# One decoder layer on one core: the gate and up products stand between the two halves of the value products

## The chip, the core and the metric

The kernel runs on one core of a Trainium2 chip. The metric is the time of one execution on the device, in microseconds (us); lower is better. Before the change it is 531.68 us, the median of three runs (531.52 to 532.6). The engines are PE (matrix products, with a weight load, PEld, that overlaps them), DVE (vector work), ACT (activation functions, copies out of PSUM), POOL (further elementwise work) and SP, which issues the DMAs. Each engine works through its own list of instructions in order and waits at semaphores for the others.

## The reference, cut to what matters

The layer has three blocks over 4 sequences of 1024 rows of 256 values. Each is normalised and added back to `x`: a gated linear scan, a cross attention of 16 heads over 64 context rows and one null row, and a feed-forward block with quantised activations and weights.

```python
x = x + attn(layernorm(x), w_qkva, gamma)
# cross attention: 16 heads of 64, keys and values from ctx (64 rows) and null_kv
sim  = einsum('bhid,bhjd->bhij', q * 64**-0.5, k)
attn = softmax(sim, axis=-1)
out  = einsum('bhij,bhjd->bhid', attn, v)  # heads joined, then @ Wout
x = x + (out - mean(out)) * rsqrt(var(out) + 1e-6) * ln_scale + ln_bias
# feed-forward, inner width 1024; bitlinear quantises both operands
z = layernorm(x)
gate, up = silu(bitlinear(z, w_gate)), bitlinear(z, w_up)
x = x + bitlinear(gate * up, w_down)
```

## The kernel before

The 4096 rows are 32 tiles of 128 rows. The first block runs in 4 groups of 4 tiles; then the keys are folded with Wq into `Mhi` and `Mlo`, and the values with Wout into `VW`. After that (from about 165 us in the profile) the cross attention and the feed-forward run together in one software pipeline, the function `stages2_3(n, u4)`, which every engine goes through for n = -2 to 38. In step n, PE does for five different tiles:

- `scores_half(n + 2, 0)` and `scores_half(n + 2, 1)`: the scores of tile n + 2, 12 matmuls of 260 columns each, into PSUM banks 0, 1 and banks 2, 3. (Line 1128 is the helper `group`, which also records gate, up and down.)
- The transposes of tile n's softmax weights `p2` into banks 4 and 5 (lines 1348 and 1356) and those of the null row's weights into bank 7 (line 1360).
- `gate_up(n, v)`: 4 matmuls of 512 columns with `wgT` into banks 0 and 1 (gate), 4 with `wuT` into banks 2 and 3 (up), for tile n - 5.
- The value products of tile n: 4 matmuls with `VW` (first half, line 1370), 4 more (second half, line 1375) and one for the null row (line 1378), all accumulated in bank 7. The profile shows each of the eight as two records, so a half is x8 there. The first half waits for `pT0_ready` and `pTn_ready`.
- In even steps a pair of transposes for a later tile (line 1261), then the down product of tile n - 7.

Around them stand, in the order of each engine's list:

- DVE in step n: the row maximum (line 984) and the subtraction (line 987) for each half of the scores of tile n + 2, the small part of the null weights of tile n (line 1045, which releases `pTn_ready`), the softmax sum of tile n + 1 (line 996), statistics (1060, 1068), then for tile n - 5 `hidden_layer` (line 1009: gate times up, waits for `silu_ready`, `zw_done` and `up_psum`), for tile n - 3 the maximum of the normalised rows (line 1074, waits for `z_ready`), the statistics of the attention output of tile n (line 1081, waits for `out_psum`), the maximum of the hidden layer (line 1016), small scale factors, and the residual of tile n - 7 (line 1027).
- ACT in step n: the copies of the transposed weights out of PSUM (737, 740, 742), the load of the Silu table (688), Silu of the gate product (line 693, waits for `gate_psum`), the quantised copy of the previous tile's hidden layer (755), the normalised rows of tile n - 3 (line 701, which releases `z_ready`), the load of the Exp table and the exponential (766).

The order is written out by hand; no scheduler stands behind it. Gate and up share their banks with the scores, so gate waits until DVE is done with the first half of the scores of tile n + 2 (`sim_sub`), and up until it is done with the second half.

Of the kernel before, what the change touches and what calls it, by code (L numbers as in the profile page):

```python
# [33 lines left out]
def decoder_layer(nc, x, ctx_in, w_qkva, gamma, Wq, Wkv, null_kv, Wout, ln_scale, ln_bias,  # L34
# [7 lines left out]
    T = B * N // P  # L42
# [17 lines left out]
    with ExitStack() as stack:  # L60
# [8 lines left out]
        def bank(b, n=512):  # L69
            return psum[:, b, 0:n]  # L70
# [268 lines left out]
        def positive(value):  # L339

            return not isinstance(value, int) or value > 0
# [18 lines left out]
        def exists(n, count):  # L360

            return not isinstance(n, int) or 0 <= n < count

        def upto(n, count):

            return min(n, count) if isinstance(n, int) else n

        def filling(n):

            return isinstance(n, int) and n < 1  # L370

        def late(n):

            return isinstance(n, int) and n >= T

        def half(n):
            return n >> 1

        def batch(n):
            b = n >> (TB.bit_length() - 1)  # L380
            return b if isinstance(b, int) else b.with_bounds(min_val=0, max_val=B - 1)
# [742 lines left out]
        def _(pe):  # L1124
            def group(dst, terms):

                for i, (lhsT, rhs) in enumerate(terms):
                    mm = pe.matmul(dst, lhsT, rhs, start=i == 0, stop=i == len(terms) - 1)  # L1128
                return mm
# [124 lines left out]
            def pair_T(q, r):  # L1254

                pe.wait_ge(xn2_ready, 2 * q + 2)
                if positive(q):
                    pe.wait_ge(xT2_lo_ready, q)
                for k in range(KD):
                    for t in range(2):  # L1260
                        mm = pe.transpose(psum[:, 6, k * 2 * P + t * P:k * 2 * P + (t + 1) * P],  # L1261
                                          xn2[:, 2 * r + t, k * P:(k + 1) * P], ident[:, :])
                mm.then_inc(xT2_psum, 1)
# [31 lines left out]
            def scores_half(n, hh, u4, q, b):  # L1295

                pe.wait_ge(xT2_lo_ready, q + 1)
                if n == 0 and hh == 1:
                    pe.wait_ge(vw_first, HC)
                    pe.wait_ge(vw_second, HC)  # L1300
                if positive(2 * n - 1 + hh):
                    pe.wait_ge(sim_sub, 2 * n - 1 + hh)
                if positive(n - 7):
                    pe.wait_ge((silu_ready, h_ready)[hh], n - 7)
                for g in (2 * hh, 2 * hh + 1):
                    mm = group(bank(g, HB * J),
                               [(xT[:, (u4 // 2) % 2, k, (u4 % 2) * P:(u4 % 2 + 1) * P],
                                 m[:, k, b, g * HB * J:(g + 1) * HB * J])
                                for k in range(KD) for xT, m in ((xT2hi, Mhi), (xT2hi, Mlo), (xT2lo, Mhi))])
                mm.then_inc(sim_psum, 1)  # L1310
# [7 lines left out]
            def gate_up(n, slot):  # L1318

                pe.wait_ge(nT_ready[slot], 16 * ((n - 5) // 2 + 1))  # L1320
                pe.wait_ge(sim_sub, upto(2 * n + 5, 2 * T))
                if positive(n - 5):
                    pe.wait_ge(silu_ready, n - 5)
                for j in range(2):
                    mm = group(bank(j), [(nT3[:, slot, k, :], wgT[:, k, j * 512:(j + 1) * 512]) for k in range(KD)])
                mm.then_inc(gate_psum, 1)
                pe.wait_ge(sim_sub, upto(2 * n + 6, 2 * T))
                if positive(n - 5):
                    pe.wait_ge(h_ready, n - 5)
                for j in range(2):  # L1330
                    mm = group(bank(2 + j), [(nT3[:, slot, k, :], wuT[:, k, j * 512:(j + 1) * 512]) for k in range(KD)])
                mm.then_inc(up_psum, 1)

            def stages2_3(n, u4):
                u, v = u4 % 2, 1 - u4 % 2
                if exists(n + 2, T):
                    scores_half(n + 2, 0, (u4 + 2) % 4, half(n + 2 - u), batch(n + 2))
                    if not filling(n):
                        scores_half(n + 2, 1, (u4 + 2) % 4, half(n + 2 - u), batch(n + 2))
                elif not late(n):  # L1340
                    gate_up(n, v)
                if exists(n, T):

                    pe.wait_ge(p_ready, 2 * n + 2)
                    if positive(n):
                        pe.wait_ge(pT0_ready, n)
                    for i in range(HC // 2):
                        mm = pe.transpose(psum[:, 4, i * P:(i + 1) * P], p2[:, u, i * P:(i + 1) * P], ident[:, :])
                    mm.then_inc(pT0_psum, 1)
                    if positive(n):  # L1350
                        pe.wait_ge(pT1_ready, n)
                    if positive(n - 7):
                        pe.wait_ge(x3_done, n - 7)
                    for i in range(HC // 2):
                        at = (HC // 2 + i) * P
                        mm = pe.transpose(psum[:, 5, i * P:(i + 1) * P], p2[:, u, at:at + P], ident[:, :])
                    mm.then_inc(pT1_psum, 1)
                    if positive(n):
                        pe.wait_ge(y2_ready, n)
                    pe.transpose(psum[0:NP, 7, D:D + P], p2[:, u, H * MK:], ident[:, :]).then_inc(pTn_psum, 1)  # L1360
                if filling(n):
                    scores_half(n + 2, 1, (u4 + 2) % 4, half(n + 2 - u), batch(n + 2))
                if exists(n + 2, T) and exists(n - 5, T):
                    gate_up(n, v)
                if exists(n, T):

                    pe.wait_ge(pTn_ready, n + 1)
                    pe.wait_ge(pT0_ready, n + 1)
                    for pair in range(HC // 2):
                        pe.matmul(bank(7, D), pT[:, pair, :], VW[:, batch(n), pair, :], start=pair == 0, stop=False)  # L1370
                if exists(n, T):

                    pe.wait_ge(pT1_ready, n + 1)
                    for pair in range(HC // 2, HC):
                        pe.matmul(bank(7, D), pT[:, pair, :], VW[:, batch(n), pair, :], start=False, stop=False)  # L1375
                    if n == 0:
                        pe.wait_ge(vwn_ready, 1)
                    pe.matmul(bank(7, D), pTn[:, :], VWnull[:, :], start=False, stop=True).then_inc(out_psum, 1)
                if u == 0 and exists(n, T - 4):
                    pair_T(half(n) + 2, u4 // 2)  # L1380
                if exists(n - 7, T):

                    pe.wait_ge(nhT_ready[v], 16 * ((n - 7) // 2 + 1))
                    pe.wait_ge(pT1_ready, upto(n + 1, T))
                    if positive(n - 7):
                        pe.wait_ge(x3_done, n - 7)
                    group(bank(5, D), [(nhT3[v][:, k, :], wdT[:, k, :]) for k in range(FC)]) \
                        .then_inc(down_psum, 1)
                if isinstance(n, int) and n >= T - 1 and exists(n - 4, T):
                    gate_up(n + 1, u)  # L1390

            steps(stages2_3)


# [22 lines left out]
```

## Time and profile before

| | before |
|---|---|
| time, median of 3 runs | 531.68 us |
| the profiled execution | 531.91 us |
| its span, first to last instruction | 530.1 us |
| PE busy | 477.0 us, 90% |
| DVE busy | 427.8 us, 81% |
| ACT busy | 325.1 us, 61% |
| POOL busy | 304.8 us, 57% |
| mean granted TensorE clock | 0.983 |

The span is the profiled execution without what lies ahead of its first and behind its last instruction, here 1.8 us. Busy is the time in which an engine executed something; the chain that ended last runs for 54% of the span over PE and for 30% over DVE, so neither alone sets the time. Times below are microseconds from the start of the span.

### The profile page before, as it was taken

Reading aid. Unit: us, or ns where it says so; the run is one execution under the profiler, and the core shown is the slowest. Engines: PE = TensorE matmul, PEld = TensorE weight load, DVE = VectorE, ACT = ScalarE, POOL = GpSimd, SP = SyncE. Lnnn points to the kernel's source line nnn. Section 1 sums busy time; section 2 is a strip of 40 time slices with the busy share of each in tenths; the row PEclk is TensorE's granted clock in tenths of the full one; section 3 lists DMA queues with packets and bytes.
Section 4 is the critical chain, followed back from the end, with each engine's and each line's share of the span. In section 5 each row is a group of like instructions: output and inputs, shape, how many; then the busy total and the mean of one; then the engine's idle time right before and its main releaser. Section 6 shows DMA issues by size and latency. Waiting matters only on the chain.

```text
span 530.1 us, 9241 instructions
## 1 busy us (share of the span) xinstructions
PE 477.0 (90%) x2926; PEld 389.5 (73%) x2954; DVE 427.8 (81%) x936; ACT 325.1 (61%) x450; POOL 304.8 (57%) x482
## 2 busy tenths in 40 slices
PE   1899999989988998999999999999999999998562
PEld 0676787767767887978887888888888878867221
DVE  4899998968527667889889889989898899886763
ACT  4433333236333434788878888888888788876450
POOL 2211233810001467788787787787877877888731
PEclk9989999999999999999999999999999999999995
DMA  8995000240000000011122122212221211122342
GB/s 263 324 350 215 1 0 1 40 80 1 1 1 1 1 1 6 6 31 36 37 54 49 39 47 45 51 36 53 44 46 36 55 41 46 38 53 51 70 100 69
DMA packets 68173, 32.06 MB, mean 60 GB/s; under 512 B 50720, under 2 KB 66336, under 8 KB 68128
## 3 DMA queue, kind: packets, MB, share of 16 engines
q1 hardware_dynamic: 68128, 31.50, 23.2%
q8 instruction: 23, 0.38, 0.3%
q14 instruction: 22, 0.18, 0.1%
HBM read 15.24 MB, written 4.19 MB: 37 GB/s over the span
## 4 chain that ended last, share of the span: by engine, by line
PE 54%; DVE 30%; issue 6%; POOL 4%; DMA 4%; ACT 1%; DVEq 1%; POOLq 0%
PE psum L1128 22%; PE psum L1370 10%; PE psum L1375 10%; DVE region_d L987 5%; DVE mx L984 4%; DVE amax L1016 3%; PE psum L1144 3%; DVE region_a L870 3%; DMA region_d<-region_d 2%; PE psum L1231 2%; PE psum L1248 1%; DVE st L1081 1%; DVE xs L812 1%; PE psum L1261 1%; DMA region_c<-region_d 1%
## 5 line engine op out<-in xcount | busy, mean ns | idle before, releaser
L523 POOL TENSOR_TENSOR region_d<-region_d,rden 128x1024 f32<-128x1024 f32 x32 | 60.9, 1903 | 90.5 <-DVE rden L1001 90.5
L1128 PE MATMUL psum<-Mhi,xT2hi 128*128 128x260 f32 x256 | 75.0, 293 | 0.2
L1128 PE MATMUL psum<-Mlo,xT2hi 128*128 128x260 f32 x256 | 72.4, 283 | 0.0
L1128 PE MATMUL psum<-Mhi,xT2lo 128*128 128x260 f32 x256 | 72.3, 283 | 0.0
L1370 PE MATMUL psum<-VW,region_d 128*128 128x256 f32 x256 | 61.1, 381 | 4.8 <-DVE pTn L1045 4.8
L1375 PE MATMUL psum<-VW,region_d 128*128 128x256 f32 x256 | 60.5, 379 | 0.0
L1370 PEld LDWEIGHTS psum<-VW,region_d 128*128 128x128 f32 x256 | 48.1, 190 | 14.9 <-DVE pTn L1045 6.4
L1375 PEld LDWEIGHTS psum<-VW,region_d 128*128 128x128 f32 x256 | 48.6, 190 | 6.6
L984 DVE TENSOR_REDUCE mx<-psum 128x8 f32<-128x520 f32 x64 | 44.2, 691 | 6.4 <-PE psum L1128 5.2
L1128 PEld LDWEIGHTS psum<-Mhi,xT2hi 128*128 128x128 f32 x256 | 48.2, 188 | 1.3 <-issue 1.0
L1128 PEld LDWEIGHTS psum<-Mlo,xT2hi 128*128 128x128 f32 x256 | 48.3, 189 | 0.0
L1128 PEld LDWEIGHTS psum<-Mhi,xT2lo 128*128 128x128 f32 x256 | 48.2, 188 | 0.0
L987 DVE TENSOR_TENSOR region_d<-psum,mx 128x520 f32<-128x520 f32 x64 | 44.8, 700 | 2.2
L1009 DVE SCALAR_TENSOR_TENSOR region_c<-psum,zw,region_c 128x1024 f32<-128x1024 f32 x32 | 41.0, 1282 | 3.6 <-ACT region_c L693 3.2
L489 POOL TENSOR_TENSOR pw_out<-pw_in,expo 128x8 f32<-128x8 f32 x8 | 13.1, 1641 | 52.4 <-DVE pw_in L804 52.4
L535 POOL CAST region_d<-region_c 128x1024 bf16<-128x1024 int16 x32 | 33.2, 1036 | 14.1 <-ACT region_c L755 14.1
L755 ACT ACTIVATE region_c<-region_c,qr 128x1024 int16<-128x1024 f32 x32 | 36.4, 1139 | 5.6 <-DVE qr L1115 5.6
L996 DVE TENSOR_REDUCE den<-region_d 128x16 f32<-128x1040 f32 x32 | 39.4, 1231 | 0.5
L1016 DVE TENSOR_REDUCE amax<-region_c 128x1 f32<-128x1024 f32 x32 | 38.2, 1193 | 0.4 <-issue 0.2
L766 ACT ACTIVATE region_d<-region_d 128x1040 f32<-128x1040 f32 x32 | 34.3, 1073 | 6.7 <-DVE region_d L987 6.4
L693 ACT ACTIVATE region_c<-psum,zw 128x1024 f32<-128x1024 f32 x32 | 35.6, 1112 | 3.6 <-PE psum L1128 3.3
L593 ACT ACTIVATE region_a<-psum 128x1024 f32<-128x1024 f32 x8 | 8.2, 1028 | 47.6 <-PE psum L1144 47.6
(140 smaller groups left out, 1219.5 us busy)
## 6 DMA issues: line engine op xcount, KB each, us to landing
out_dram<-xs SPq DMA_DIRECT2D x32, 128.0 KB, 1.9
xs<-in_x_dram SPq DMA_DIRECT2D x1, 2560.0 KB, 13.5
VW<-in_L_xattn_Wkv_dram SPq DMA_DIRECT2D x1, 2048.0 KB, 12.1
region_b<-in_L_xattn_Wkv_dram SPq DMA_DIRECT2D x1, 2048.0 KB, 17.3
xs<-in_x_dram SPq DMA_DIRECT2D x3, 512.0 KB, 6.8
region_w<-in_L_ffn_w_gate_dram SPq DMA_DIRECT2D x2, 512.0 KB, 9.8
region_w<-in_L_ffn_w_up_dram SPq DMA_DIRECT2D x2, 512.0 KB, 7.8
region_w<-in_L_ffn_w_down_dram SPq DMA_DIRECT2D x8, 128.0 KB, 5.7
```

Source lines behind the costliest of these rows:

```text
L523: pool.tensor_tensor(p2[:, v, 0:H * MK].rearrange("p (h j) -> p h j", j=MK), e[:, :, 0:MK], rden[:, v, :].unsqueeze(2).broadcast_to([P, H, ...
L693: act.activation(hid3[v], banks(0, 2).rearrange("p b n -> p (b n)"), ACT.Silu, scale=zw[:, (n - 5) % 4, 0:1]).then_inc(silu_ready, 1)
L755: act.activation(nq3, hid3[u], ACT.Copy, scale=qr[:, u, 0:1]).then_inc(hq_done, 1)
L766: act.activation(e2[:, u, :], e2[:, u, :], ACT.Exp).then_inc(exp_done, 1)
L984: dve.tensor_reduce(mx[:, hh, :].rearrange("p (b h) -> p b h", h=HB), scores, AX.X, ALU.max) \
L987: dve.tensor_tensor(e2[:, u, hh * 2 * HB * J:(hh + 1) * 2 * HB * J].rearrange("p (b h j) -> p b h j", b=2, j=J), scores, mx[:, hh, :].rear ...
L996: dve.tensor_reduce(den[:, :], e2[:, slot, :].rearrange("p (h j) -> p h j", j=J), AX.X, ALU.add) \
L1009: dve.scalar_tensor_tensor(out=hid3[v], in0=banks(2, 2).rearrange("p b n -> p (b n)"), scalar=zw[:, (n - 5) % 4, 1:2], in1=hid3[v], op0=AL ...
L1016: dve.tensor_reduce(amax[:, v, 0:1], hid3[v], AX.X, ALU.max, apply_absolute_value=True) \
L1128: mm = pe.matmul(dst, lhsT, rhs, start=i == 0, stop=i == len(terms) - 1)
L1370: pe.matmul(bank(7, D), pT[:, pair, :], VW[:, batch(n), pair, :], start=pair == 0, stop=False)
L1375: pe.matmul(bank(7, D), pT[:, pair, :], VW[:, batch(n), pair, :], start=False, stop=False)
```

## The change

`gate_up` of step n moves behind the first four value products. It now stands between the two halves. The condition on it stays: it is issued there in the steps in which tile n + 2 and tile n - 5 both exist, n = 5 to 29, which are 25 steps. The waits inside `gate_up` and those of the value products stay as they are. Accumulation in bank 7 stays open across gate and up, which write banks 0 to 3.

```diff
                 if filling(n):
                     scores_half(n + 2, 1, (u4 + 2) % 4, half(n + 2 - u), batch(n + 2))
-                if exists(n + 2, T) and exists(n - 5, T):
-                    gate_up(n, v)
                 if exists(n, T):
 
                     pe.wait_ge(pTn_ready, n + 1)
                     pe.wait_ge(pT0_ready, n + 1)
                     for pair in range(HC // 2):
                         pe.matmul(bank(7, D), pT[:, pair, :], VW[:, batch(n), pair, :], start=pair == 0, stop=False)
+                if exists(n + 2, T) and exists(n - 5, T):
+                    gate_up(n, v)
                 if exists(n, T):
 
                     pe.wait_ge(pT1_ready, n + 1)
```

The list of PE in one of these steps before, from the null row's transpose to its value product (`wgT` is gate, `wuT` up, `VW` the values; what a matmul waits for stands behind it):

```order
L1360 MATMUL psum<-ident,region_d 80x128 [waits y2_ready]
L1128 MATMUL psum<-wgT,region_d 128x512 [waits silu_ready,sim_sub,nT_ready1]
L1128 MATMUL psum<-wgT,region_d 128x512 x3
L1128 MATMUL psum<-wuT,region_d 128x512 [waits h_ready,sim_sub]
L1128 MATMUL psum<-wuT,region_d 128x512 x3
L1370 MATMUL psum<-VW,region_d 128x256 [waits pT0_ready,pTn_ready]
L1370 MATMUL psum<-VW,region_d 128x256 x3
L1375 MATMUL psum<-VW,region_d 128x256 [waits pT1_ready]
L1375 MATMUL psum<-VW,region_d 128x256 x3
L1378 MATMUL psum<-VWnull,pTn 128x256
```

The same place of the changed kernel:

```order
L1360 MATMUL psum<-ident,region_d 80x128 [waits y2_ready]
L1368 MATMUL psum<-VW,region_d 128x256 [waits pT0_ready,pTn_ready]
L1368 MATMUL psum<-VW,region_d 128x256 x3
L1128 MATMUL psum<-wgT,region_d 128x512 [waits silu_ready,sim_sub,nT_ready1]
L1128 MATMUL psum<-wgT,region_d 128x512 x3
L1128 MATMUL psum<-wuT,region_d 128x512 [waits h_ready,sim_sub]
L1128 MATMUL psum<-wuT,region_d 128x512 x3
L1375 MATMUL psum<-VW,region_d 128x256 [waits pT1_ready]
L1375 MATMUL psum<-VW,region_d 128x256 x3
L1378 MATMUL psum<-VWnull,pTn 128x256
```

The first value products, with their waits, moved ahead of gate and up; nothing else moved on PE, and line 1370 is line 1368 now.

The lists of DVE, ACT, POOL and SP are the same in both kernels. DVE's, from the subtraction of the scores' second half to the statistics of the attention output, before and after alike:

```order
L987 TENSOR_TENSOR region_d<-psum,mx 128x520 [waits max_done]
L1045 TENSOR_TENSOR pTn<-psum,pTn 16x128 [waits pTn_hi]
L996 TENSOR_REDUCE den<-region_d 128x16 [waits exp_done]
L1060 BN_STATS st<-xs 128x6 [waits nmr4_done,x2_done,consts_set]
L1001 RECIPROCAL rden<-den 128x16 [waits den_done]
L1068 BN_AGGR mv<-st 128x2 [waits st4_done,consts_set]
L1009 SCALAR_TENSOR_TENSOR region_c<-psum,zw,region_c 128x1024 [waits silu_ready,zw_done,up_psum]
L1074 TENSOR_REDUCE amax<-region_d 128x1 [waits z_ready]
L1081 BN_STATS st<-psum 128x6 [waits out_psum,consts_set]
L1087 BN_AGGR mv<-st 128x2 [waits st3_done,consts_set]
```

Nothing moved there: PE's value products wait for the second of these rows, and three later rows wait for ACT (`silu_ready`, `z_ready`) and PE (`up_psum`, `out_psum`).

## Rows read from the trace of the kernel before

**Rows 1.** The page's head: the span of the profiled execution.
```profile
span 530.1 us, 9241 instructions
```

**Rows 2.** Busy time by stretch; the decimal behind POOL's count is PEclk.
```profile
238.00:466.00 228.00, 224.45 (x1463) 192.10 (x1483) 205.58 (x426) 191.69 (x248) 182.56 (x307) 1.00 0.21 45
...
486.00:495.00 9.00, 7.11 (x41) 4.99 (x39) 6.20 (x19) 4.61 (x7) 6.96 (x15) 1.00 0.24 54
495.00:505.00 10.00, 5.58 (x22) 2.39 (x24) 7.65 (x18) 4.46 (x6) 7.20 (x14) 0.84 0.41 90
```

**Rows 3.** Waits from 300 to 480 us: total, times, longest.
```profile
DVE st L1081 <- PE psum L1378: 6.9, 17, 0.9
```

**Rows 4.** Timeline of PE, one step: start, us, then the instruction.
```profile
330.53 0.81 PE L1128 MATMUL psum<-wgT,region_d 128*128 128x512 bf16 x3
...
331.52 1.04 PE L1128 MATMUL psum<-wuT,region_d 128*128 128x512 bf16 x4 [0.18 <-DVE region_d L987]
...
332.39 1.89 PE L1370 MATMUL psum<-VW,region_d 128*128 128x256 f32 x8
...
334.12 1.89 PE L1375 MATMUL psum<-VW,region_d 128*128 128x256 f32 x8
...
335.66 0.47 PE L1378 MATMUL psum<-VWnull,pTn 80*128 80x256 f32 x1
...
337.19 0.36 PE L1128 MATMUL psum<-Mhi,xT2hi 128*128 128x260 f32 x1
...
340.03 0.28 PE L1128 MATMUL psum<-Mhi,xT2lo 128*128 128x260 f32 x1
...
341.02 0.27 PE L1360 MATMUL psum<-ident,region_d 128*80 128x128 f32 x1
```

**Rows 5.** Timeline of DVE, the same step and part of the next.
```profile
331.49 0.28 DVE L1045 TENSOR_TENSOR pTn<-psum,pTn 16x128 fp32r<-16x128 f32 x1
...
333.83 1.28 DVE L1009 SCALAR_TENSOR_TENSOR region_c<-psum,zw,region_c 128x1024 f32<-128x1024 f32 x1 [0.17 <-ACT region_c L693]
...
335.25 0.42 DVE L1074 TENSOR_REDUCE amax<-region_d 128x1 f32<-128x256 f32 x1
...
336.23 0.43 DVE L1081 BATCH_NORM_STATS2 st<-psum 128x6 f32<-128x256 f32 x1 [0.56 <-PE psum L1378]
...
340.42 0.69 DVE L984 TENSOR_REDUCE mx<-psum 128x8 f32<-128x520 f32 x1
...
341.88 0.28 DVE L1045 TENSOR_TENSOR pTn<-psum,pTn 16x128 fp32r<-16x128 f32 x1
...
346.70 0.43 DVE L1081 BATCH_NORM_STATS2 st<-psum 128x6 f32<-128x256 f32 x1 [0.20 <-PE psum L1378]
```

**Rows 6.** Timeline of ACT, the same step.
```profile
331.29 1.28 ACT L688 ACT_TABLE_LOAD   x1
...
332.58 1.11 ACT L693 ACTIVATE region_c<-psum,zw 128x1024 f32<-128x1024 f32 x1
```

**Rows 7.** Timeline of PE near the end, where it had waited.
```profile
476.70 1.99 PE L1370 MATMUL psum<-VW,region_d 128*128 128x256 f32 x8 [0.68 <-DVE pTn L1045]
...
478.53 1.89 PE L1375 MATMUL psum<-VW,region_d 128*128 128x256 f32 x8
...
507.34 1.04 PE L1128 MATMUL psum<-wgT,region_d 128*128 128x512 bf16 x4 [0.58 <-DMA region_d<-region_c]
```

**Rows 8.** Timeline of ACT near the end, where it waited for gate.
```profile
508.41 1.11 ACT L693 ACTIVATE region_c<-psum,zw 128x1024 f32<-128x1024 f32 x1 [1.74 <-PE psum L1128]
```

**Rows 9.** Timeline of DVE, tile 30.
```profile
476.36 0.28 DVE L1045 TENSOR_TENSOR pTn<-psum,pTn 16x128 fp32r<-16x128 f32 x1 [1.23 <-ACT pTn L740]
...
480.80 0.42 DVE L1074 TENSOR_REDUCE amax<-region_d 128x1 f32<-128x256 f32 x1
...
481.14 0.42 DVE L1081 BATCH_NORM_STATS2 st<-psum 128x6 f32<-128x256 f32 x1
```

**Rows 10.** Timeline of DVE, tile 5, the first step that changes.
```profile
217.11 0.28 DVE L1045 TENSOR_TENSOR pTn<-psum,pTn 16x128 fp32r<-16x128 f32 x1
```

## The prediction

> **What bounds the kernel now.** I read the busy time by stretch first, because it says whether one engine alone sets the pace. In the steady part PE is busy for 224.45 of 228.00 us, DVE for 205.58 [rows 2], so PE looks like the bound, at the full granted clock (1.00, the 2.4 GHz level). The span of the profiled execution is 530.1 us [rows 1] and its time 531.9 us, 0.2 us from the median of 531.68. Next the waits: DVE, in every one of 17 steps, waits for the end of the value products, 6.9 us in total, 0.4 us a step [rows 3]. So DVE and PE release each other in turn, and I need the order in time rather than busy shares.
>
> The timelines of one step give it. I count from the start of DVE's small instruction on the null weights (line 1045), T = 331.49, the one that frees the first value products; it starts again at 341.88, a step of 10.39 us [rows 5]. In between:
>
> - Gate starts on PE at 330.53, before T, while DVE is still at the second half of the scores. Up waits for that half and starts at 331.52; the first value products at 332.39, the second at 334.12, the null product at 335.66 [rows 4]. So gate fills time in which PE has to wait for DVE anyway.
> - ACT loads the Silu table from 331.29 for 1.28 us and starts Silu at 332.58, right behind the load [rows 6]. Gate had long been done: Silu is held by ACT's own list.
> - DVE's hidden layer starts at 333.83 after 0.17 us of waiting for Silu; the row maximum of line 1074 at 335.25, the statistics of the attention output (line 1081) at 336.23, after waiting 0.56 us for the null product [rows 5]. From there DVE needs 341.88 - 336.23 = 5.65 us to the next T.
>
> Line 1081 starts 336.23 - 331.49 = 4.74 us after T here, and 346.70 - 341.88 = 4.82 us in the next step [rows 5]; the mean is 4.78 us. The step is that plus the 5.65 us behind it.
>
> **The change part by part.** No work is added or removed. Three things move.
>
> *The first value products go ahead of gate and up.* Their wait for DVE's line 1045 now stands ahead of gate too. Queued behind it on PE are gate, up, the second half, down and the next scores; ACT's Silu and DVE's hidden layer wait for them. After a wait for T they start 476.70 - 476.36 = 0.34 us behind it [rows 7, 9], instead of 0.90 us as now (332.39 - 331.49) [rows 4, 5]. That alone is a gain of 0.56 us for them.
>
> *Gate loses its cover.* The transposes end at 341.02 + 0.27 = 341.29 and T is at 341.88 [rows 4, 5]; PE has nothing to do in between, until 342.22. Gate and up then stand behind the first half. After a wait, the first half takes 478.53 - 476.70 = 1.83 us, a tenth more than without one [rows 7]. Gate starts at 0.34 + 1.83 = 2.17 us after T. Up takes 332.39 - 331.52 = 0.87 us, and gate has the same shape and count [rows 4], so up starts at 3.04, the second half at 3.91, the null product 335.66 - 334.12 = 1.54 us later, at 5.45, and line 1081 could start 336.23 - 335.66 = 0.57 us behind that, at 6.02 [rows 4, 5].
>
> *Silu comes later, and with it a row of DVE work that stands ahead of line 1081.* Where Silu really waits for gate, it starts 508.41 - 507.34 = 1.07 us behind gate's first matmul [rows 7, 8]. So Silu starts at 2.17 + 1.07 = 3.24 us after T, against 332.58 - 331.49 = 1.09 now [rows 5, 6]. The table load is hidden then. ACT does Silu, the quantised copy and the normalised rows in one go, and DVE's line 1074 comes 335.25 - 332.58 = 2.67 us behind Silu's start [rows 5, 6]: at 5.91. Line 1081 can follow it by 481.14 - 480.80 = 0.34 us [rows 9], at 6.25. This is later than PE's 6.02, so the hidden branch ends last and the wait for the null product goes away; its successor is a wait of the hidden layer for Silu of about two microseconds.
>
> Line 1081 moves from 4.78 to 6.25 us after T: +1.47 us. Behind it DVE's 5.65 us stay as they are, if PE's scores are in time. The null product to the first score is 337.19 - 335.66 = 1.53 us and to the end of the last score 340.03 + 0.28 - 335.66 = 4.65 us [rows 4], in a step with the pair of transposes, the longer kind. So the scores end at 5.45 + 4.65 = 10.10 us after T, and DVE comes to the second maximum at 6.25 + 340.42 - 336.23 = 10.44 [rows 5]. That holds, with 0.34 us of slack. The new step is 6.25 + 5.65 = 11.90 us.
>
> The moved order stands in 25 steps, n = 5 to 29, now from 217.11 to 476.36 [rows 9, 10]. 25 x 1.47 = 36.8 us. In step 5 the quantised copy between Silu and the normalised rows does not exist yet; there PE's own path decides, about 0.4 us less. Sum: +36.4 us, and nothing behind step 29 makes up for it, since the later steps' gate and up are issued elsewhere and DVE's chain hands the delay on. 531.9 + 36.4 = 568.3 us for the profiled execution, and with its 0.2 us to the median **568 us**.
>
> What the trace cannot show is a gate product directly behind half of an open accumulation in another bank. From below it costs nothing, as between up and the value products now. From above I take the tenth that a wait before the first half costs, twice a step and for the handover to Silu once: 0.3 x 25 = 7.5 us, so 576. The value I take is nothing, because up to value products shows none: 0.87 us for four matmuls, in both steps. At the lower end, if the hidden branch were faster than I count it, PE's 6.02 would decide: 25 x (6.02 - 4.78) = 31 us, 563.
>
> The clock needs a word of its own. After the change PE stands still from the end of the transposes to the first value products: 11.90 + 0.34 - (5.45 + 341.29 - 335.66) = 1.16 us a step [rows 4], so it is busy for some 90%. The trace has a stretch in which PE is busy for 7.11 of 9.00 us at a granted clock of 1.00, and only with 5.58 of 10.00 us does it fall, to 0.84 [rows 2]. By these rows the clock stays and the sum stays 568. A rule of the Trainium skill speaks against it: "TensorE: Matmul & The Clock Gate", section "A second HAM failure mode: psum-queue depth-cycling", says that frequent short idle times between groups of matmuls, with the output going from bank to bank, can make the clock swing between its two levels. By that rule the time would be that of the last rival below; the trace, with waits at up and at line 1370 in several steps and a clock of 1.00, doesn't bear it out so far.
>
> **The rivals.**
>
> 1. *Only the value products count.* Silu's lateness is absorbed and line 1081 is set by PE, 6.02 us after T: 563 us, with the range of small deviations 556 to 564. For it: PE is the engine that DVE waits for today [rows 3]. Against it: lines 1009 and 1074 stand ahead of 1081 on DVE, and the distance from Silu to 1074 is ACT's own busy time.
>
> 2. *More than the chain.* Another queue that is near its limit moves in, at most likely the scores: slack 0.34 us against DVE. If these handovers cost 0.3 us and more a step, the time is 576, up to 590. For it: several engines wait in turn. Against it: ACT and POOL are busy for 191.69 and 182.56 of 228 us [rows 2], and what follows line 1081 moves with it.
>
> 3. *Not slower.* PE does the same work, and two small waits go, those of gate and up for the scores' halves: up waited 0.18 us in the step shown [rows 4]. If PE alone set the pace, the step would fall by up to that: 25 x 0.18 = 4.5 us, 527. The place is the first value products' wait, and it decides from the point at which DVE's line 1045 has ended when PE ends the transposes. Now it ends at 341.88 + 0.28 = 342.16, the transposes at 341.29 [rows 4, 5]: 0.87 us too late. DVE can't be earlier, since both maximum and subtraction of the second half (1.46 us, from 340.42 to 341.88) come only after the last score has ended at 340.31, and the transposes need just 0.98 us from there. So I hold this for hardly possible.
>
> 4. *The clock falls.* If PE ran at the lower level, its 11.90 - 1.16 = 10.74 us of a step would take twice that. In one step of ten, this is 2.5 x 10.74 = 27 us more, 595; in all 25 steps it is over 800. For it speaks the new idle time in each step, against it the stretch with less work at 1.00 [rows 2].
>
> **How the numbers follow.** Forecast, 564 to 572 us: 0.67. Rival 1, 556 to 564: 0.14. Rival 2: 0.13. Rival 3: 0.04, half of it a gain and half no difference. Rival 4: 0.02. What a measurement of this kernel can tell from no change is 0.2%, or 1.1 us. Slower thus holds 0.96, faster 0.02, the same 0.02. The range is 560 to 575 us: it takes in the forecast's case, the better part of rival 1 with its 563, and the lower part of rival 2 up to just under its 576.
>
> **What would show it.** In the profile after, in steps 5 to 29: the step is 11.9 us instead of 10.4; the first value products start 0.34 us behind line 1045, with an idle time of about 1.2 us put down to DVE; Silu has an idle time ahead of it, put down to PE's gate, and starts 3.2 us after T; line 1009 waits for Silu some 2 us in each step; line 1081 waits for nothing or for very little; PE's clock stays at 1.00. I am wrong if the first value products start without waiting (then rival 3), if line 1081 still waits for the null product in most steps (rival 1), if the line 984 maximum waits for the scores (rival 2), or if the clock falls in the steady part (rival 4).

## The result, and the profile after

| | before | after |
|---|---|---|
| median time | 531.87 us (4 runs) | 573.72 us (4 runs) |
| profiled execution, its span | 531.91, 530.1 us | 575.26, 573.4 us |
| PE busy | 477.0 us, 90% | 487.6 us, 85% |
| DVE busy | 427.8 us, 81% | 427.3 us, 75% |

The changed kernel is slower: ratio 1.0773, 95% interval 1.0736 to 1.081. The forecast was 568 us in a range of 560 to 575. The direction, the mechanism and the size of the steps without the pair of transposes were right; the steps with the pair are longer than forecast. The median is 5.7 us above the forecast and lies in the range, but above the 564 to 572 us that had most of the chances, and two of the four runs (575.15 and 575.26 us) lie just above 575.

The span rose by 43.3 us. DVE's busy time is the same and PE's grew by 10.6 us, so most of the rise is waiting. The waits of the changed kernel between 320 and 500 us (who waited for whom: total, times, longest):

```profile
ACT region_c L693 <- PE psum L1128: 30.9, 15, 2.7
DVE region_c L1009 <- ACT region_c L693: 29.8, 15, 2.3
...
PE psum L1368 <- DVE pTn L1045: 18.8, 15, 1.9
```

Silu waits for gate, DVE's hidden layer waits for Silu, and PE's first value products wait for DVE's line 1045: fifteen times each, a ring of three engines. DVE's wait of line 1081 for PE [rows 3] is not among them any more.

One step on PE and the head of the next, a step without the pair of transposes and one with it (start, us, instruction, idle time before):

```profile
387.66 1.99 PE L1368 MATMUL psum<-VW,region_d 128*128 128x256 f32 x8 [0.86 <-DVE pTn L1045]
...
390.35 1.03 PE L1128 MATMUL psum<-wuT,region_d 128*128 128x512 bf16 x4
391.22 1.89 PE L1375 MATMUL psum<-VW,region_d 128*128 128x256 f32 x8
392.76 0.47 PE L1378 MATMUL psum<-VWnull,pTn 80*128 80x256 f32 x1
...
399.53 2.00 PE L1368 MATMUL psum<-VW,region_d 128*128 128x256 f32 x8 [1.56 <-DVE pTn L1045]
...
404.63 0.47 PE L1378 MATMUL psum<-VWnull,pTn 80*128 80x256 f32 x1
405.62 0.66 PE L1261 MATMUL psum<-ident,region_d 128*128 128x128 f32 x4 [0.52 <-ACT region_d L658]
...
409.75 0.28 PE L1128 MATMUL psum<-Mhi,xT2lo 128*128 128x260 f32 x1
```

The same steps on DVE:

```profile
387.32 0.28 DVE L1045 TENSOR_TENSOR pTn<-psum,pTn 16x128 fp32r<-16x128 f32 x1
...
393.23 0.42 DVE L1074 TENSOR_REDUCE amax<-region_d 128x1 f32<-128x256 f32 x1
393.56 0.42 DVE L1081 BATCH_NORM_STATS2 st<-psum 128x6 f32<-128x256 f32 x1
...
399.19 0.28 DVE L1045 TENSOR_TENSOR pTn<-psum,pTn 16x128 fp32r<-16x128 f32 x1
...
405.44 0.42 DVE L1081 BATCH_NORM_STATS2 st<-psum 128x6 f32<-128x256 f32 x1
...
408.63 0.70 DVE L984 TENSOR_REDUCE mx<-psum 128x8 f32<-128x520 f32 x1 [0.27 <-PE psum L1128]
...
410.07 0.70 DVE L984 TENSOR_REDUCE mx<-psum 128x8 f32<-128x520 f32 x1
...
411.54 0.28 DVE L1045 TENSOR_TENSOR pTn<-psum,pTn 16x128 fp32r<-16x128 f32 x1
```

And on ACT, Silu of the first step and the rows for the pair of transposes in the second:

```profile
390.56 1.11 ACT L693 ACTIVATE region_c<-psum,zw 128x1024 f32<-128x1024 f32 x1 [1.66 <-PE psum L1128]
...
404.97 0.59 ACT L658 ACTIVATE region_d<-xs,nmr,rstd 128x256 f32<-128x256 f32 x1
```

With T = 387.32, the first half starts at 0.34, up at 3.03, the second half at 3.90, the null product at 5.44, Silu at 3.24, line 1074 at 5.91 and line 1081 at 6.24, against 4.74 in [rows 5]. The next T is at 11.87. All of these are within 0.03 us of the forecast. The next step, however, takes 411.54 - 399.19 = 12.35 us. Its line 1081 is at 6.25 as well; but the pair of transposes waits 0.52 us for ACT's line 658, the scores end later (the last one starts at 409.75), and DVE waits 0.27 us for their first half at 408.63 and starts the second maximum at 410.07, 10.88 us after T. Such a step comes every second time from step 8 to step 26, ten times in all.

The clock after, in the steady stretch and in the ramp (busy time of PE, PEld, DVE, ACT, POOL, then PEclk):

```profile
230.00:520.00 290.00, 252.72 (x1585) 207.46 (x1610) 224.15 (x465) 210.42 (x273) 202.51 (x338) 1.00 0.20 38
...
173.00:176.00 3.00, 3.00 (x18) 2.92 (x17) 0.74 (x2) 1.24 (x3) 0.00 (x0) 0.69 0.00 0
```

And in the ramp of the kernel before:

```profile
173.00:176.00 3.00, 3.00 (x18) 2.71 (x17) 2.25 (x3) 0.52 (x2) 0.00 (x0) 1.00 0.00 0
```

In the steady stretch PE keeps its full clock. In the ramp, where the changed kernel runs the same instructions as the one before, the profiled execution of after had a dip that the one of before did not have. It does not go with the change. In the profiles of all ten kernels of this case PE stands still for 2.06 to 2.08 us and starts again near 171 us, in code that is the same in all of them. Behind it the granted clock stayed at 1.00 in five of them (the kernel before and four of the experiments), and step 5 started at 216.90 to 217.16 us; in the other five the clock fell to the 1.2 GHz level for some microseconds, and step 5 started at 218.55 to 218.96 us.

### The profile page after: what moved, and what is told of

It is laid out like the page before. It is cut to its first block, busy times and chain, and to the rows that moved or that the text cites. A ratio compares the mean times of both kernels' runs of the same rounds, so it can differ in the third digit from the quotient of the medians.

```text
span 573.4 us, 9241 instructions
## 1 busy us (share of the span) xinstructions
PE 487.6 (85%) x2926; PEld 390.7 (68%) x2954; DVE 427.3 (75%) x936; ACT 324.1 (57%) x450; POOL 305.9 (53%) x482
## 4 chain that ended last, share of the span: by engine, by line
PE 39%; DVE 32%; issue 12%; ACT 10%; DMA 4%; POOL 3%; DVEq 1%; POOLq 0%; SPq 0%; ACTq 0%
PE psum L1128 16%; PE psum L1368 11%; DVE mx L984 7%; DVE region_d L987 6%; ACT region_c L755 5%; PE psum L1144 4%; DVE amax L1016 3%; DVE region_a L870 2%; ACT region_d L701 2%; PE psum L1375 2%; DMA region_d<-region_d 2%; PE psum L1261 2%; DVE pTn L1045 2%; PE psum L1231 1%; PE psum L1248 1%
## 5 line engine op out<-in xcount | busy, mean ns | idle before, releaser
L1368 PE MATMUL psum<-VW,region_d 128*128 128x256 f32 x256 | 63.7, 392 | 36.2 <-DVE pTn L1045 36.2
L1368 PEld LDWEIGHTS psum<-VW,region_d 128*128 128x128 f32 x256 | 46.0, 189 | 49.2 <-DVE pTn L1045 44.3
L1375 PE MATMUL psum<-VW,region_d 128*128 128x256 f32 x256 | 60.5, 379 | 0.0
L1375 PEld LDWEIGHTS psum<-VW,region_d 128*128 128x128 f32 x256 | 48.6, 190 | 8.9
L1144 PE MATMUL psum<-xT1hi,w1hi 128*128 128x512 f32 x96 | 32.6, 421 | 4.1 <-DVE region_a L870 2.9
```

The source lines that it names most:

```text
L1144: mm = pe.matmul(bank(b), lhsT, rhs, start=i == 0, stop=i == len(terms) - 1)
```

## The experiments

Steps are counted from DVE's line 1045 (T), as in the prediction. Ratios are to the kernel before, from runs on the same chip.

**Gate ahead of the value products, but behind their wait.** This takes gate's cover away and leaves Silu early. The edit, in the kernel before:

```diff
                 if exists(n + 2, T) and exists(n - 5, T):
+                    pe.wait_ge(pTn_ready, n + 1)
+                    pe.wait_ge(pT0_ready, n + 1)
                     gate_up(n, v)
```

> The order of the kernel before (gate, up, both halves of the value products), but gate waits for what the first half waits for, DVE's line 1045. So gate loses its cover and Silu does not come late. My theory (two parts: gate behind the wait, and the late hidden branch): gate 0.34 us after T, up 1.21, first half 2.08, second 3.81, null product 5.35, line 1081 at 5.92 us after T; step 5.92 + 5.65 = 11.57 us, no extra in even steps; 25 x (5.92 - 4.78) = 28.5 us over before, 560 us. A rival by which the loss comes from Silu alone (PE's list may wait, since it has gaps): 532 to 535 us.

Measured: 560.01 us, ratio 1.0514 (1.0497 to 1.0532). On PE:

```profile
343.96 1.04 PE L1128 MATMUL psum<-wgT,region_d 128*128 128x512 bf16 x4 [1.33 <-DVE pTn L1045]
```

and on DVE, where line 1380 is the null product:

```profile
343.62 0.28 DVE L1045 TENSOR_TENSOR pTn<-psum,pTn 16x128 fp32r<-16x128 f32 x1
...
349.54 0.43 DVE L1081 BATCH_NORM_STATS2 st<-psum 128x6 f32<-128x256 f32 x1 [1.41 <-PE psum L1380]
...
355.19 0.28 DVE L1045 TENSOR_TENSOR pTn<-psum,pTn 16x128 fp32r<-16x128 f32 x1
```

Gate starts 0.34 us after T, line 1081 is at 5.92 and the step is 11.57 us, in both kinds of step. Here line 1074 is early (4.09 us after T), and DVE waits 1.41 us for the null product: PE's path decides. So gate and up behind the wait for DVE cost 27 us in this order, with Silu early, against the 42 us of the change.

**Up alone between the halves.** The edit, in the kernel before, with `gate_up` cut in two functions:

```diff
                 if exists(n + 2, T) and exists(n - 5, T):
-                    gate_up(n, v)
+                    gate_only(n, v)
...
                         pe.matmul(bank(7, D), pT[:, pair, :], VW[:, batch(n), pair, :], start=pair == 0, stop=False)
+                if exists(n + 2, T) and exists(n - 5, T):
+                    up_only(n, v)
```

> Half of the change: gate stays ahead of the value products, up alone goes between the halves. My theory: gate keeps its cover, the first half starts 0.34 us after T, up 2.17, the second half 3.04, the null product 4.58, line 1081 at 5.15 us after T, by PE; Silu stays at about 1.1 to 1.5 us. The hidden layer waits for up and starts at about 3.25. Step 5.15 + 5.65 = 10.8 us; 25 x 0.37 = 9 us over before, 541 us. A rival by which opening the accumulation of bank 7 for other banks' products costs by itself (any split of the halves): the second half comes later than 0.87 us behind up, and the time is 550 us or more.

Measured: 541.55 us, ratio 1.0159 (1.0136 to 1.0182). DVE:

```profile
347.93 0.28 DVE L1045 TENSOR_TENSOR pTn<-psum,pTn 16x128 fp32r<-16x128 f32 x1
...
353.08 0.43 DVE L1081 BATCH_NORM_STATS2 st<-psum 128x6 f32<-128x256 f32 x1 [0.30 <-PE psum L1388]
...
358.71 0.28 DVE L1045 TENSOR_TENSOR pTn<-psum,pTn 16x128 fp32r<-16x128 f32 x1
```

Line 1081 is at 5.15 us after T and the step is 10.78 us, as expected. The second half starts 0.86 us behind up, so an open accumulation with other banks' products in between costs nothing by itself here. The 9 us are up's 0.87 us behind the wait and 0.1 us for a first half that follows a wait, less the 0.56 us by which this half now starts earlier. All that the changed kernel costs beyond them needs gate behind the wait too.

**The pair's rows ahead of Silu.** The edit, in the changed kernel:

```diff
+                if exists(n, T - 5) or n == -1:
+                    act.wait_ge(xT2_psum, (n + 1) // 2 + 1)
+                    norm2(n + 5, (n + 5) % 4)
                 if exists(n - 5, T):
                     silu_gate(n, v)
```

with the same three lines taken out behind `norm3(n, v)`.

> The changed kernel, but ACT makes the normalised rows that PE's pair of transposes (line 1261) waits for ahead of Silu, while it waits for gate, not behind it. My theory of the 0.47 us that even steps take more than odd ones: PE waits for these rows since Silu is late, so the scores end late. Then even steps fall from 12.34 to 11.87 us, ten of them: 4.7 us less than the changed kernel, which is 568 us or so against its 572.3 to 575.3. Rival: the even steps are longer for the pair of transposes themselves (0.43 us of PE work): no change, 573 us, and even steps stay at 12.3.

Measured: 570.0 us, ratio 1.0705 (1.0684 to 1.0727); the intervals of the two ratios do not overlap. PE, where a pair of transposes follows the null product:

```profile
376.34 0.47 PE L1378 MATMUL psum<-VWnull,pTn 80*128 80x256 f32 x1
376.65 0.60 PE L1261 MATMUL psum<-ident,region_d 128*128 128x128 f32 x4
```

The wait is gone, and steps with and without the pair take 11.88 us alike; the profiled execution took 567.92 us. Steps 5 to 29 take 295.20 us together, against 299.73 in the changed kernel: 4.5 us less, where 4.7 were expected. The median came down by 3.7 us, with the four runs between 567.92 and 570.98.

**Both rows ahead of Silu.** As above, and `norm3(n, v)` moved there too, ahead of the three lines.

> The changed kernel, but ACT makes both normalised rows (for line 1074 and for PE's pair of transposes) ahead of Silu. Line 1074 then waits only for the hidden layer: 5.69 us after T instead of 5.91, line 1081 at 6.03 instead of 6.25, where PE's own path allows it too. My theory (the hidden branch ends last by 0.23 us, and the even steps' extra is the wait for the pair's rows): all steps 11.68 us, 25 x 0.22 = 5.5 us less than with the pair's rows alone early (570.0), 564.5 us. Rival (the value products' end sets line 1081 anyway): no change from 570.0.

Measured: 563.27 us, ratio 1.0584 (1.0562 to 1.0607). DVE:

```profile
368.07 0.28 DVE L1045 TENSOR_TENSOR pTn<-psum,pTn 16x128 fp32r<-16x128 f32 x1
...
373.75 0.41 DVE L1074 TENSOR_REDUCE amax<-region_d 128x1 f32<-128x256 f32 x1
374.08 0.43 DVE L1081 BATCH_NORM_STATS2 st<-psum 128x6 f32<-128x256 f32 x1
...
379.72 0.28 DVE L1045 TENSOR_TENSOR pTn<-psum,pTn 16x128 fp32r<-16x128 f32 x1
```

Line 1074 is at 5.68, line 1081 at 6.01 and the step is 11.65 us. This is the other part of the theory: in the changed kernel the hidden branch ends after the value products, by 0.23 us a step. Both row makers together are worth 10 us. What is left, 31 us over before, is gate and up behind the wait in the changed kernel's own order.

**Gate and up behind all the value products.** `gate_up` stands right behind the null product.

> Gate and up behind all the value products. My theory (the hidden branch ends last, through Silu, line 701 and line 1074, which stand ahead of line 1081 on DVE): null product 3.70, gate 4.03, Silu 5.10, line 1074 at 7.77, line 1081 at 8.11 us after T; steps of 13.8 us and, in even steps, some 0.4 us more: 573 + 25 x 1.9 = 620 us. Rival (the value products' end sets line 1081, as in the kernel before): line 1081 at 4.28 us after T, steps of under 10.4 us or PE's own 10.3, 520 to 530 us.

Measured: 656.13 us in a single run, which bears no interval. DVE's line 1045, a step without the pair and one with it, and line 1081 of the first:

```profile
401.32 0.28 DVE L1045 TENSOR_TENSOR pTn<-psum,pTn 16x128 fp32r<-16x128 f32 x1
...
409.43 0.42 DVE L1081 BATCH_NORM_STATS2 st<-psum 128x6 f32<-128x256 f32 x1
...
415.06 0.28 DVE L1045 TENSOR_TENSOR pTn<-psum,pTn 16x128 fp32r<-16x128 f32 x1
...
432.06 0.28 DVE L1045 TENSOR_TENSOR pTn<-psum,pTn 16x128 fp32r<-16x128 f32 x1
```

Steps without the pair take 13.74 us, as expected. Those with it take 17.0, not 14.2. The waits of PE (300 to 500 us), and the clock over the same stretch and in a step with the pair:

```profile
PE psum L1368 <- DVE pTn L1045: 19.0, 13, 2.2
PE psum L1261 <- ACT region_d L658: 16.5, 7, 2.4
```

```profile
300.00:500.00 200.00, 158.05 (x897) 125.94 (x896) 123.27 (x255) 116.18 (x152) 109.67 (x182) 0.90 0.15 31
415.00:420.00 5.00, 4.60 (x11) 3.67 (x12) 2.17 (x6) 0.33 (x1) 3.46 (x4) 0.50 0.14 39
```

PE waits up to 2.2 us for DVE and up to 2.4 us for the pair's rows. Behind the longer waits for DVE, ahead of the steps with the pair, the granted clock of the value products is 0.50, the 1.2 GHz level; behind the shorter ones (0.86 us) it is 1.00. The rival (520 to 530 us) has fallen: with the null product done 3.71 us after T, line 1081 still came at 8.11, because lines 1009 and 1074 stand ahead of it. My time was 36 us too low: ten steps with the pair were 2.8 us longer each than I had expected, and steps 6, 28 and 29 were longer too, all of them steps in which the clock fell.

**The same with the pair's rows early**, to see which idle time brings the clock down.

> Gate and up behind all the value products, and the rows for PE's pair of transposes made ahead of Silu. In the kernel without the second edit the odd steps came out at 13.74 us as expected, but the even ones at 17.0 with the granted clock at 0.88 to 0.90, where PE waited over 2 us for these rows. If that wait brings the clock down, both go: even steps as long as odd ones, 13.74 us, clock about 1.00 between 230 and 560 us, 25 steps x 13.74 + 218 + 54 = 616 us. If the clock falls for the idle time ahead of the value products or for the order alone, it stays under 0.95 and the time over 640 us.

Measured: 643.41 us, in a single run. Waits of PE and the clock, 300 to 500 us:

```profile
PE psum L1368 <- DVE pTn L1045: 30.3, 14, 2.2
PE psum L1356 <- DVE xs L1027: 12.1, 14, 1.4
```

```profile
300.00:500.00 200.00, 157.61 (x895) 126.36 (x894) 126.93 (x266) 117.80 (x156) 113.97 (x191) 0.91 0.16 33
```

The first value products of two steps, behind the same wait:

```profile
274.53 1.99 PE L1368 MATMUL psum<-VW,region_d 128*128 128x256 f32 x8 [2.17 <-DVE pTn L1045]
...
304.02 3.78 PE L1368 MATMUL psum<-VW,region_d 128*128 128x256 f32 x8 [2.17 <-DVE pTn L1045]
```

The first theory was wrong: the wait for the pair's rows is gone, and the clock is still 0.91, with steps of 13.74, 15.2 and 15.4 us mostly in turn. But the wait ahead of the value products does not decide by itself either. It is 2.2 to 2.4 us long in each of steps 6 to 29; behind it the clock stayed at 1.00 in 8 of these 24 steps, and the first half took 1.99 us, while in 16 it fell, and the half took up to 3.78 us. In the changed kernel the longest such wait is 1.9 us and the clock stays at 1.00. What exactly makes the difference these runs don't settle.

**The hidden layer's maximum first.** The wait of DVE at line 1081 in the kernel before could be filled. The edit, in the kernel before, on DVE:

```diff
+                if not late(n) and exists(n - 5, T):
+                    hidden_max(n, v)
                 if exists(n, T):
 
                     count, = registers(dve, n + 1)
                     dve.wait_ge(consts_set, 2)
                     dve.wait_ge(out_psum, count)
```

with the two lines taken out two blocks below.

> The kernel before, but DVE takes the maximum of the hidden layer (line 1016, 1.2 us) ahead of the statistics of the attention output (line 1081), for whose input it waits 0.2 to 0.6 us in each step; PE's order is that of before. By my reading of before (DVE's 5.65 us behind line 1081 and PE's 4.78 us ahead of it release each other in turn) the wait disappears and PE's own work decides, 10.47 and 10.04 us in turn: 10.25 instead of 10.44 us a step, 25 steps: 4.7 us less, 527 to 528 us. Rival: line 1081 comes about 0.6 us later after T, and through POOL and ACT the copies of the next transposes with it: no change or slower, 532 to 545 us.

Measured: 530.84 us against 532.57, ratio 0.9961 (0.9945 to 0.9977): faster by 0.4%, some 40% of what I expected. The waits, 300 to 480 us:

```profile
ACT region_d L681 <- POOL sc L547: 10.0, 10, 1.4
...
DVE mx L984 <- PE psum L1128: 3.0, 7, 0.4
PEld psum L1261 <- ACT region_d L658: 2.1, 7, 0.3
```

DVE's line 1045 at both ends of a step with the pair:

```profile
351.42 0.28 DVE L1045 TENSOR_TENSOR pTn<-psum,pTn 16x128 fp32r<-16x128 f32 x1
...
362.09 0.28 DVE L1045 TENSOR_TENSOR pTn<-psum,pTn 16x128 fp32r<-16x128 f32 x1
```

DVE's wait at line 1081 is gone, but steps with the pair take 10.67 us and not 10.47, the others 10.06. ACT's waits for POOL have grown from 5.3 to 10.0 us, and new are those of PE for ACT's rows for the pair and of DVE for the scores behind them.

**The same, and the pair's rows at the head of ACT's step.** The three lines of `norm2` move ahead of `norm_out(n, v)`.

> The faster kernel of before (the hidden layer's maximum ahead of line 1081), and ACT makes the rows for PE's pair of transposes at the head of its step, while it waits for POOL, not behind line 701. In the kernel without the second edit, steps with the pair take 10.67 us and the others 10.06; PE waits there up to 0.3 us for these rows and DVE up to 0.4 us for the scores behind them. If these waits go with the edit, the pair's steps take 10.35 to 10.4: ten times 0.3 = 3 us less, 528 us against 530.8 (and 532.6 before). Rival: the rows now delay line 681 and the copies of the transposes by 0.5 us on ACT: no change or slower, 531 to 535 us.

Measured: 529.62 us against 532.69, ratio 0.9938 (0.9916 to 0.996). Line 1045 again, a step with the pair:

```profile
350.92 0.28 DVE L1045 TENSOR_TENSOR pTn<-psum,pTn 16x128 fp32r<-16x128 f32 x1
...
361.37 0.28 DVE L1045 TENSOR_TENSOR pTn<-psum,pTn 16x128 fp32r<-16x128 f32 x1
```

Steps with the pair take 10.45 us, the others 10.08. Of the 0.3 us that I expected in a step with the pair, 0.2 came: PE's wait for the rows is gone, but DVE still waits 0.2 us for the scores. This is the fastest kernel of the case, by 0.6% over the one before; that it beats the kernel with the first edit alone is likely (in the profiled steps it does by 0.2 us in two), but their intervals overlap.

## Why the prediction was right, and where it fell short

*What bounds the kernel.* Right: PE and DVE release each other. Line 1081 minus T plus 5.65 us gave the length of the steps in the kernel before and in all seven with its order of DVE's list, to 0.05 us, wherever nothing came late behind it. In steps 5, 6 and 29 it is 0.4, 0.4 and 1.5 us less, in 9 and 23 some 0.3 us more, in the kernel before as in the others.

*The first value products go first.* Right: 0.34 us after T, 1.83 us long after a wait, and a wait put down to line 1045.

*Gate loses its cover.* Right in size: 11.57 us a step with the wait ahead of gate, and only 10.78 where gate stays covered. The gate product behind half of an open accumulation costs nothing by itself, as I had taken it: up starts 3.03 us after T, where I had 3.04.

*Silu comes late and ends last.* Right: 3.24, 5.91 and 6.24 us; taking it off gave back the 0.23 us by which it passed PE's path.

*"Behind it DVE's 5.65 us stay as they are, if PE's scores are in time."* This is the step that fell short. I counted the scores from the null product with no wait ahead of the pair of transposes. But the pair needs rows that ACT makes behind line 701, in line 658. In the kernel before, in the step of [rows 5, 6]:

```profile
335.12 0.59 ACT L658 ACTIVATE region_d<-xs,nmr,rstd 128x256 f32<-128x256 f32 x1
```

They are done at 335.71, 0.05 us behind the start of the null product (335.66) and 3.13 us behind the start of Silu, and PE starts the pair at 335.96, without a wait. With Silu 2.15 us later after T, the same 3.13 us put the end of the rows at 6.37 us after T, while PE comes to the pair 0.30 us behind the null product, at 5.75. So the trace of before already held this wait of 0.6 us, and I left it out. Measured, the rows end 6.37 us after T (405.56 - 399.19) and the pair starts at 6.43. The last score ends at 410.03, 10.84 us after T and not 10.10, which is 0.74 us late against a slack of 0.34; with the handover to the second maximum the step came out at 12.35 us, where I had 11.90. Against the steps without the pair it is 0.47 us, in ten steps 4.7 us; making the rows early gave back 4.5. Rival 2 had named the place, the scores, without the cause. The two timelines differ in steps 5 to 29 by what these rows say:

```profile
218.96 0.28 DVE L1045 TENSOR_TENSOR pTn<-psum,pTn 16x128 fp32r<-16x128 f32 x1
```

```profile
518.69 0.28 DVE L1045 TENSOR_TENSOR pTn<-psum,pTn 16x128 fp32r<-16x128 f32 x1 [1.23 <-ACT pTn L740]
```

518.69 - 218.96 = 299.73 us against 476.36 - 217.11 = 259.25 [rows 9, 10]: +40.5 us, where I had +36.4. Of these 4.1 us the ten longer steps make 4.7; the rest of the steps come to 0.6 us less than in my sum. Of the remaining rise of the span, 43.3 - 40.5 = 2.8 us, 1.85 lie ahead of step 5, most of it in the clock's dip, and 1 us lies behind step 29, where the mean granted clock is 0.82 instead of 0.86. The dip is not part of the change: two of the four runs of the changed kernel came at 572.3 us with a mean clock of 0.985, two at 575.2 with 0.977. The two faster ones are 40.4 us over before, which is what steps 5 to 29 add; by their clock they ran without the dip, though no trace of them shows it.

*The clock.* Right in outcome, 1.00, but my evidence was weaker than I took it for. A short stretch with PE busy for 7.11 of 9.00 us at 1.00 [rows 2] tells little: with gate last, PE was busy for 158 of 200 us, the same share, and the clock was 0.90. So the forecast's evidence would have allowed a clock of 1.00 for those kernels too. The Trainium skill's "TensorE: Matmul & The Clock Gate", section "A second HAM failure mode: psum-queue depth-cycling", which the prediction cites, describes such a swing between the two levels. In these two kernels the trace agrees that the clock swings (0.50 in one stretch, 0.90 and 0.91 on average), but not that frequent short waits are enough: in the changed kernel PE waits in every step too, and the clock stays at 1.00.

*The rivals.* The first (only the value products count) is refuted by the two kernels with line 1074 moved one way or the other. The second (more than the chain) is the one that held in part: the time lies between the forecast's case and its 576, and its sign, a wait of line 984 for the scores, is there in every second step. The range held because it reached into this rival. The third (not slower) is refuted: PE waited for line 1045 in every step, 0.86 and 1.56 us in the two shown. The fourth (the clock falls) did not happen in the changed kernel's steady part.

## What to carry to other kernels

Before moving work on an engine that waits in turn with another, ask what it does while that engine waits: work moved from ahead of a wait to behind it is paid for, even on an engine that is 98% busy. The price is the time of the work less what it already ran beyond the wait: gate and up take 1.74 us, the value products had started 0.56 us later than the wait asked for, and with both behind the wait and Silu early line 1081 came 1.14 us later. Then follow each engine that the moved work feeds to the end of its own list, not only to the first result that is missed: here ACT's Silu carried two further rows with it, one that cost 0.23 us in every step and one that cost 0.47 us in every second step. A slack is only as good as the list of waits that was counted in it.

## What was not expected of the hardware

With gate and up last, PE waited up to 2.2 us ahead of the value products, and a second time in some steps for up to 2.4 or 1.4 us, and the granted clock was 0.90 and 0.91 over 200 us; in the changed kernel, with waits of up to 1.9 us, it was 1.00. The cost was larger than the waits: steps of 17.0 instead of the 14.2 us expected at the full clock.

Nor does the length of one wait tell what the clock will do. Behind the same 2.2 us it stayed at 1.00 in 8 of 24 steps of one execution and fell in 16, and behind the same standstill of 2.1 us near 170 us it fell in five of ten profiled executions and stayed in five. In these the dip made step 5 start some 1.8 us later, so part of the difference between single executions is this, and not the kernel.
